# Graph attention on one core: exponentials behind a group's last round, the last head's products divided, four statistics in the MLP

## The chip, the cores and the metric

One core of a Trainium2 chip runs the whole program in one launch. The metric is the device time of one execution in microseconds (us); lower is better. The core has five engines with a queue of instructions each: TensorE (PE in the profile; PEld is its weight load), VectorE (DVE), ScalarE (ACT), GpSimd (POOL) and SyncE (SP, which issues loads). Each engine works off its queue in order and waits at semaphores for the others.

## The reference

The program computes a small transformer over a graph of 1250 nodes with 512 features, and then one graph aggregation:

```
for i in range(4):                          # layers
    y = cond_layer_norm(x, cond, s1, b1)    # (x-mu)*rsqrt(var+eps)*(1+scale)+bias, scale and bias from cond
    q, k, v = y@wq+bq, y@wk+bk, y@wv+bv     # 4 heads of 128
    scores = sum(q[src]*k[dst]); attn = softmax over the edges of each src
    x = x + (segment_sum(attn*v[dst], src) @ wo + bo)
    y = cond_layer_norm(x, cond, s2, b2)
    x = x + relu(y@m_w1+m_b1)@m_w2 + m_b2
x = layernorm(x0 + x)
x = layernorm(x + segment_sum(x[src]*edge_weight, dst) @ weight.T)
```

## The kernel before

The 1250 nodes are padded to NT = 10 tiles of 128. The edges are first turned into two dense tables of 10 x 128 x 1250: edge weights, and the logarithms of edge counts (an absent edge gets a huge negative value). Attention is then dense: for each head and each tile of 128 rows, scores against all 1250 nodes, plus the table's row (`Lr`, loaded by an issue of ScalarE's queue), then exp. Products in full precision are made of three matmuls each (`mm3`): operands are kept as a rounded high part and a low part, so each operand that is made on the way passes ScalarE, which writes the high part (`_hi`), and VectorE, which subtracts and writes the low part (`_lo`).

A layer is: normed and turned rows with queries, keys and values; attention, 4 heads h of GROUPS = 5 groups g of two tiles; the MLP, 5 chunks c of two tiles. Three layers run in a hardware loop, the fourth is written out behind it. There is no scheduler: in each engine's function `layer` the order of its work is written out by hand.

In group g of head h, all engines go through five rounds r:

- TensorE: `turn` transposes four 128x128 blocks of the two probability tiles (`prob`) into PSUM bank 5 or 6. Rounds 0 and 1 are the first tile's blocks 0 to 7, round 2 holds blocks 8 and 9 of both tiles, rounds 3 and 4 are the second tile's 0 to 7. Between the rounds stand the scores of the next group's two tiles (`scores_a`), the next head's queries and keys in a head's last group (`qk`), or, in the last head's last group, only two small conditioning products (`cond`). Also between rounds are the two output projections (`project`, j = 0 and 1) of the group before, at rounds 0 and 2.
- ScalarE: `pt_hi_` writes PT_hi of each round; `exp` of the next tiles; `o_hi_`.
- VectorE: `pt_lo_` writes PT_lo of each round; `mask` (i) adds the table to the scores of tile i and finds the maximum, at rounds 1 and at the end; `recip` (i) after exp (i); `add_wo` adds a projected tile to x; `o_lo_`.
- Before the rounds, TensorE does `out_heads` of the group before: the product of values and the turned probabilities, ten source tiles d of three matmuls, in the order 8, 9, 0 to 7, as PT_lo of rounds 2, 3 and 4 comes. It writes bank 7, from which `o_hi_` and `o_lo_` make the operand of `project`, which writes bank 7 too. `take_m` makes each next user of bank 7 wait for the one before: `out_heads` for the last `add_wo`, the second `project` for the first's `add_wo`.

A score's tile i = 10 h + 2 g + 2 is the first one of the next group, i - 1 the second one of this group. Transposes of round 0 wait for the exponential of a group's first tile, those of round 2 for its second. Transposes of round r also wait for PT_lo of round r - 2, for the bank.

The lines of the profile: L1479 the transposes, L1299 all `mm3` products (told apart by names: PT and v in `out_heads`, k and q in scores, wo and oT in `project`, mw in the MLP), L697 PT_hi, L1087 PT_lo, L1071 mask, L686 exp, L1077 and L1079 recip, L702 and L1091 `o_hi_` and `o_lo_`, L1101 `add_wo`. In the last group of the last head, VectorE also makes the first two normed tiles for the MLP: `center` (L1015) and `norm` (L1022). The statistics of each tile of x (`stats`, L1044 and L1047) are followed by `rsqrt` on GpSimd (L537, L539), and `norm` needs both.

Of the kernel before, what the change touches and what calls it, by code (L numbers as in the profile page):

```python
# [27 lines left out]
NT = -(-N // P)  # L28
# [4 lines left out]
H = 4  # L33
# [74 lines left out]
    o_ready=H * GROUPS, o_hi=H * GROUPS, o_split=H * GROUPS,  # L108
# [8 lines left out]
def build(nc, T, out):  # L117
    ctx = ExitStack()
    with ctx:
# [357 lines left out]
        def _(pool):  # L477
# [48 lines left out]
            def layer(l, ahead):  # L526
# [41 lines left out]
                for h in range(H):  # L568
                    for g in range(GROUPS):
# [3 lines left out]
                        if h == H - 1 and g:  # L573
                            rsqrt(NT + 2 * g - 2)
                            rsqrt(NT + 2 * g - 1)
                for n in range(2):
                    rest(MLP2 + n)
                rsqrt(2 * NT - 2)
                rsqrt(2 * NT - 1)
                for c in range(GROUPS):  # L580
                    h_rest(c, 0)
                    h_rest(c, 1)
                    if c == 0:
# [29 lines left out]
        def _(act):  # L613
# [48 lines left out]
            def layer(l, ahead):  # L662
# [28 lines left out]
                def pt_hi_(h, g, r):  # L691
                    n = (GROUPS * h + g) * 5 + r
                    wait("turned", n + 1)
                    if r == 0:
                        wait("o_ready", GROUPS * h + g)
# [52 lines left out]
                for h in range(H):  # L748
                    for g in range(GROUPS):
                        last, more = g == GROUPS - 1, h < H - 1  # L750
                        i = NT * h + 2 * g + 2
                        if g:
                            o_hi_(h, g - 1)
                            exp(i - 1)
                        for r in range(5):
                            pt_hi_(h, g, r)
                            if g == 0 and r == 0 and h:
# [3 lines left out]
                            if r == 2 and not last:  # L761
                                exp(i)
                            for n in pieces(h, g, r):
                                piece_hi(n)
                    if h < H - 1:
# [54 lines left out]
        def _(dve):  # L820
# [210 lines left out]
            def layer(l, ahead):  # L1031
# [100 lines left out]
                for h in range(H):  # L1132
                    for g in range(GROUPS):
                        last, more = g == GROUPS - 1, h < H - 1
                        i = NT * h + 2 * g + 2
                        if g:
                            o_lo_(h, g - 1)
                            recip(i - 1)
                        elif h:
                            mask(i - 1)  # L1140
                        for r in range(5):
                            pt_lo_(h, g, r)
                            if last and not more:
                                if r in (0, 3):
                                    center(NT + r // 3)
                                if r in (1, 4):
                                    norm(NT + r // 3)
                            if last and more:
# [3 lines left out]
                            if r in (0, 2):  # L1152
# [4 lines left out]
                            if r == 2 and not last:  # L1157
                                recip(i)
# [4 lines left out]
                        if g and not more:  # L1163
# [13 lines left out]
                for t in (NT - 2, NT - 1):  # L1177
                    stats(NT + t)
                for c in range(GROUPS):
                    if c < GROUPS - 1:  # L1180
                        for n in (NT + 2 * c + 2, NT + 2 * c + 3):
# [3 lines left out]
                            if n + 1 < 2 * NT:  # L1185
                                norm(n + 1)
                    elif ahead:
# [109 lines left out]
        def _(pe):  # L1297
# [108 lines left out]
            def layer(l, ahead):  # L1406
# [76 lines left out]
                def out_heads(h, g, parts):  # L1483
                    order = (8, 9, 0, 1, 2, 3, 4, 5, 6, 7)
                    if 0 in parts:
                        take_m("o_split", GROUPS * h + g + 1)
                    for d in [d for part in parts for d in order[5 * part:5 * part + 5]]:
# [4 lines left out]
                    if 1 in parts:  # L1492
                        m.then_inc(S["o_ready"], 1)

# [63 lines left out]
                for h in range(H):  # L1558
                    for g in range(GROUPS):
# [3 lines left out]
                        if g:  # L1563
                            out_heads(h, g - 1, (0, 1))
# [145 lines left out]
```

## Time and profile before

| what | before |
|---|---|
| median of 3 runs | 2042.48 us (2041.83 to 2045.47) |
| the profiled execution | 2040.49 us |
| its span, first to last instruction | 2038.7 us |
| granted TensorE clock, mean | 0.981 |
| TensorE matmuls busy | 1800.9 us, 88% |
| VectorE busy | 1332.7 us, 65% |
| ScalarE busy | 909.0 us, 45% |
| GpSimd busy | 391.5 us, 19% |

The span is what the trace covers; 1.8 us of the execution lie around it. Busy shares are means over the whole program. The rows that matter are those of single stretches. A timeline's row that ends in [x <-engine tile line] says that the engine stood idle for x us before it and what released it; neighbours on one engine overlap by some 0.1 us, so a step from start to start is a little shorter than the busy time.

### The profile page before, as it was taken

The page shows a single profiled execution, that of the slowest core. Times are in us where ns is not written, and L with a number is a line of the kernel's source. Part 1 is how long each engine was busy: PE and PEld are TensorE (multiplying, and loading weights), DVE is VectorE, ACT ScalarE, POOL GpSimd, SP SyncE. Part 2 cuts the span into 40 slices and gives each one's busy share as a digit, 9 for nine tenths or more (in the row PEclk, how much of TensorE's full clock was granted, in tenths as well). Part 3 has the DMA queues.
Part 4 walks back from the last instruction along what each step waited for, and adds up shares of the span by engine and source line. Part 5 has one row for each costly group of instructions (what it writes and reads, how often), then busy time and mean ns, then how long its engine had stood idle before and what let it go on. Part 6 is the DMA issues. An engine that isn't in the chain of part 4 may idle for free.

```text
span 2038.7 us, 35054 instructions
## 1 busy us (share of the span) xinstructions
PE 1800.9 (88%) x12603; PEld 1568.6 (77%) x12603; DVE 1332.7 (65%) x2447; ACT 909.0 (45%) x1525; POOL 391.5 (19%) x469
## 2 busy tenths in 40 slices
PE   1566359999999999999999999999999999999898
PEld 0455348988878789888787888887888988878777
DVE  8899955576685556766855567568555676685644
ACT  2798534454453244544532345445324454453221
POOL 5322223000024230000252200001523000023301
PEclk9999769999999999999999999999999999999999
DMA  1300352242231022432310224223101242232122
GB/s 23 108 0 0 135 202 78 77 140 87 84 122 46 17 67 85 133 96 82 118 52 16 66 87 130 88 88 122 53 15 58 85 136 93 81 121 88 38 66 73
DMA packets 62769, 165.95 MB, mean 81 GB/s; under 512 B 5777, under 2 KB 23986, under 8 KB 62605
## 3 DMA queue, kind: packets, MB, share of 16 engines
q10 hardware_dynamic: 23040, 102.41, 15.2%
q1 hardware_dynamic: 39572, 61.45, 9.6%
q8 instruction: 97, 1.59, 0.3%
q14 instruction: 60, 0.49, 0.1%
HBM read 146.58 MB, written 17.02 MB: 80 GB/s over the span
## 4 chain that ended last, share of the span: by engine, by line
PE 61%; issue 15%; DVE 13%; ACT 6%; DVEq 2%; DMA 1%; ACTq 1%; POOL 0%; POOLq 0%
PE ps L1299 55%; PE ps L1479 4%; DVE PT_lo L1087 3%; ACT PT_hi L697 3%; ACT prob L686 2%; PE ps L1401 2%; DVE prob L1071 2%; DVEq L934 1%; DVE CW L945 1%; DVE x L1101 1%; DVE CW L948 1%; DVE onehot L906 1%; DVE CW L992 1%; PE ps L1670 0%; DVE cpart L895 0%
## 5 line engine op out<-in xcount | busy, mean ns | idle before, releaser
L1087 DVE TENSOR_TENSOR PT_lo<-ps,PT_hi 128x512 fp32r<-128x512 f32 x400 | 271.1, 688 | 33.9 <-ACT PT_hi L697 17.0
L686 ACT ACTIVATE prob<-prob,nmax 128x1250 f32<-128x1250 f32 x160 | 214.2, 1338 | 176.6 <-DVE nmax L1071 176.6
L697 ACT ACTIVATE PT_hi<-ps 128x512 fp32r<-128x512 f32 x400 | 231.4, 590 | 69.3 <-PE ps L1479 69.2
L1479 PE MATMUL ps<-ident,prob 128*128 128x128 f32 x1600 | 244.1, 275 | 15.3 <-DVE PT_lo L1087 13.4
L1071 DVE CUSTOM_DVE_ANT_0 prob<-ps,Lr 128x1250 f32<-128x1250 f32 x160 | 232.5, 1453 | 35.5 <-PE ps L1299 31.8
L1299 PE MATMUL ps<-PT_hi,v_hi 128*128 128x256 f32 x800 | 233.0, 291 | 19.8 <-DVE PT_lo L1087 19.8
L1479 PEld LDWEIGHTS ps<-ident,prob 128*128 128x128 f32 x1600 | 182.7, 140 | 64.4 <-DVE PT_lo L1087 47.7
L1299 PE MATMUL ps<-PT_lo,v_hi 128*128 128x256 f32 x800 | 225.8, 282 | 0.0
L1299 PE MATMUL ps<-PT_hi,v_lo 128*128 128x256 f32 x800 | 225.7, 282 | 0.0
L1299 PE MATMUL ps<-k_hi,q_hi 128*128 128x512 f32 (+2 forms) x480 | 191.7, 399 | 0.5
L1299 PE MATMUL ps<-yT_hi,wqk_hi 128*128 128x256 f32 x640 | 184.7, 289 | 0.0
L1299 PE MATMUL ps<-yT_hi,wqk_lo 128*128 128x256 f32 x640 | 181.0, 283 | 0.0
L1299 PE MATMUL ps<-yT_lo,wqk_hi 128*128 128x256 f32 x640 | 180.8, 283 | 0.0
L1299 PEld LDWEIGHTS ps<-PT_hi,v_hi 128*128 128x128 f32 x800 | 152.4, 190 | 33.0 <-DVE PT_lo L1087 33.0
L1299 PE MATMUL ps<-k_lo,q_hi 128*128 128x512 f32 (+2 forms) x480 | 169.4, 353 | 0.0
L1299 PE MATMUL ps<-k_hi,q_lo 128*128 128x512 f32 (+2 forms) x480 | 169.4, 353 | 0.0
L1299 PE MATMUL ps<-win,onehot 128*128 128x128 bf16 x1680 | 105.7, 222 | 64.3 <-DVE CW L948 56.6
L1299 PEld LDWEIGHTS ps<-win,onehot 128*128 128x128 bf16 x1680 | 96.3, 99 | 74.5 <-DVE CW L948 65.9
L1299 PEld LDWEIGHTS ps<-PT_hi,v_lo 128*128 128x128 f32 x800 | 152.6, 191 | 0.0
L1299 PEld LDWEIGHTS ps<-PT_lo,v_hi 128*128 128x128 f32 x800 | 152.6, 191 | 0.0
L544 POOL TENSOR_TENSOR wo_lo<-piece,wo_hi 128x512 fp32r<-128x512 f32 x16 | 20.6, 1290 | 675.8 <-ACT wo_hi L728 675.8
L1053 DVE SCALAR_TENSOR_TENSOR q_lo<-ps,bias,q_hi 128x256 fp32r<-128x256 f32 x80 | 38.8, 484 | 148.2 <-ACT k_hi L676 148.2
(209 smaller groups left out, 4287.8 us busy)
## 6 DMA issues: line engine op xcount, KB each, us to landing
Lr<-l_table ACTq DMA_DIRECT2D x160, 625.0 KB, 3.8
piece<-in_L_gnn_m_w_dram SPq DMA_DIRECT2D x32, 256.0 KB, 2.7
w_table<-CW SPq DMA_DIRECT2D x1, 6250.0 KB, 17.7
l_table<-CW SPq DMA_DIRECT2D x10, 625.0 KB, 7.0
prob<-w_table SPq DMA_DIRECT2D x10, 625.0 KB, 3.9
x<-in_x_dram SPq DMA_DIRECT2D x2, 2304.0 KB
piece<-in_L_gnn_wv_dram SPq DMA_DIRECT2D x16, 256.0 KB, 2.8
piece<-in_L_gnn_wq_dram SPq DMA_DIRECT2D x16, 256.0 KB, 4.4
```

Of the source, the lines that this page charges most:

```text
L544: pool.tensor_tensor(lo, raw, hi.bitcast(F32), ALU.subtract).then_inc(S["piece_split"], 1)
L686: act.activation(buf, buf, ACT.Exp, bias=nmax[:, i % 4:i % 4 + 1], scale=-1.0, accum_out=rsum[:, i % 4:i % 4 + 1]).then_inc(S["exped"], 1)
L697: act.activation(o, i, ACT.Copy).then_inc(S["pt_hi"], 1)
L906: m = dve.tensor_scalar(onehot[:, j % SBUFS, b, :], iota_h[:], eT[:, 0, b, group], None, ALU.is_equal)
L934: base = dve.value_load(grow_i[0:1, bass.ds(i * UNROLL_G + j, 1)], min_val=0, max_val=N - WIN)
L945: dve.tensor_tensor(only, only, sums[:, 2], ALU.add).then_inc(e_chain, 1)
L1053: m = dve.scalar_tensor_tensor(out=lo[:, pair(c)], in0=bank(b, i * PAIR, (i + 1) * PAIR), scalar=bias[:, i, h:h + 1], in1=hi[:, pair(c)].b ...
L1071: dve.tensor_tensor_reduce(prob[:, i % 3, 0:N], ps[:, off:off + N], Lr[:, i % LBUFS, 0:N], -SCALE, BIG, ALU.add, ALU.min, nmax[:, i % 4:i ...
L1087: dve.tensor_tensor(lo, i, hi.bitcast(F32), ALU.subtract).then_inc(S["pt_split"], 1)
L1299: return pe.matmul(o, a, b, start=start, stop=stop)
L1401: m = pe.transpose(bank(5 + n % 2, k * P, (k + 1) * P), y[:, k * P:(k + 1) * P], ident[:])
L1479: m = pe.transpose(bank(5 + n % 2, at * P, (at + 1) * P), prob[:, (NT * h + 2 * g + j) % 3, d * P:(d + 1) * P], ident[:])
```

## The change

In an attention group, ScalarE's exponential of the next group's first tile moves from behind round 2 to behind round 4, and the exponential of the group's own second tile goes ahead of `o_hi_`. VectorE makes both reciprocals at the start of the group that uses the tiles, ahead of `o_lo_`. In the last group of the last head, `out_heads` of the group before is made in three parts, in the order 0 to 9, ahead of rounds 0, 1 and 2; a new semaphore, `o_part`, lets `pt_hi_` of rounds 0 and 1 overwrite what the first two parts have read. `o_hi_` and `o_lo_` then follow round 2, the projections follow rounds 2 and 3, and `add_wo` rounds 3 and 4. The statistics of the last four tiles of x, with their `rsqrt`, move from attention's end into the MLP's first two chunks. Elsewhere `out_heads` only takes its list of tiles in another form.

```diff
--- before.py
+++ after.py
@@ -105,7 +105,7 @@
     v_ready=NT, v_hi=NT, v_split=NT,
     scores_ready=H * NT, masked=H * NT, exped=H * NT, recip_ready=H * NT, 
     turned=H * GROUPS * 5, pt_hi=H * GROUPS * 5, pt_split=H * GROUPS * 5,
-    o_ready=H * GROUPS, o_hi=H * GROUPS, o_split=H * GROUPS,
+    o_ready=H * GROUPS, o_part=2, o_hi=H * GROUPS, o_split=H * GROUPS,
     wo_ready=H * NT, x_added=H * NT, bo_added=NT,
     bn_done=2 * NT, centered=2 * NT, inverted=H * NT, var_eps=2 * NT, h_ready=2 * GROUPS, h_relu=2 * GROUPS, h_split=2 * GROUPS,
     m2_ready=NT, x_mlp=NT,
@@ -570,16 +570,17 @@
                         for r in range(5):
                             for n in pieces(h, g, r):
                                 rest(n)
-                        if h == H - 1 and g:
+                        if h == H - 1 and 0 < g < GROUPS - 1:
                             rsqrt(NT + 2 * g - 2)
                             rsqrt(NT + 2 * g - 1)
                 for n in range(2):
                     rest(MLP2 + n)
-                rsqrt(2 * NT - 2)
-                rsqrt(2 * NT - 1)
                 for c in range(GROUPS):
                     h_rest(c, 0)
                     h_rest(c, 1)
+                    if c < 2:
+                        rsqrt(2 * NT - 4 + 2 * c)
+                        rsqrt(2 * NT - 3 + 2 * c)
                     if c == 0:
                         for n in range(2, KT):
                             rest(MLP2 + n)
@@ -691,7 +692,12 @@
                 def pt_hi_(h, g, r):
                     n = (GROUPS * h + g) * 5 + r
                     wait("turned", n + 1)
-                    if r == 0:
+                    if h == H - 1 and g == GROUPS - 1:
+                        if r < 2:
+                            wait("o_part", r + 1)
+                        elif r == 2:
+                            wait("o_ready", GROUPS * h + g)
+                    elif r == 0:
                         wait("o_ready", GROUPS * h + g)
                     o, i = round_view(PT_hi, n, r)
                     act.activation(o, i, ACT.Copy).then_inc(S["pt_hi"], 1)
@@ -750,18 +756,21 @@
                         last, more = g == GROUPS - 1, h < H - 1
                         i = NT * h + 2 * g + 2
                         if g:
-                            o_hi_(h, g - 1)
                             exp(i - 1)
+                            if more or not last:
+                                o_hi_(h, g - 1)
                         for r in range(5):
                             pt_hi_(h, g, r)
+                            if last and not more and r == 2:
+                                o_hi_(h, g - 1)
                             if g == 0 and r == 0 and h:
                                 exp(i - 1)
                             if last and more:
                                 qk_hi_(h + 1, r)
-                            if r == 2 and not last:
-                                exp(i)
                             for n in pieces(h, g, r):
                                 piece_hi(n)
+                        if not last:
+                            exp(i)
                     if h < H - 1:
                         exp(NT * (h + 1))
                         o_hi_(h, GROUPS - 1)
@@ -1134,8 +1143,10 @@
                         last, more = g == GROUPS - 1, h < H - 1
                         i = NT * h + 2 * g + 2
                         if g:
-                            o_lo_(h, g - 1)
+                            recip(i - 2)
                             recip(i - 1)
+                            if more or not last:
+                                o_lo_(h, g - 1)
                         elif h:
                             mask(i - 1)
                         for r in range(5):
@@ -1145,22 +1156,24 @@
                                     center(NT + r // 3)
                                 if r in (1, 4):
                                     norm(NT + r // 3)
+                                if r == 2:
+                                    o_lo_(h, g - 1)
+                                if r > 2:
+                                    add_wo(h, 2 * g - 5 + r)
                             if last and more:
                                 qk_lo_(h + 1, r)
                             if g == 0 and r == 1:
                                 recip(i - 1)
-                            if r in (0, 2):
+                            if r in (0, 2) and not (last and not more):
                                 if g:
                                     add_wo(h, 2 * g - 2 + r // 2)
                                 elif h:
                                     add_wo(h - 1, NT - 2 + r // 2)
-                            if r == 2 and not last:
-                                recip(i)
                             if r == 1 and not last:
                                 mask(i)
                         if not last:
                             mask(i + 1)
-                        if g and not more:
+                        if g and not last and not more:
                             stats(NT + 2 * g - 2)
                             stats(NT + 2 * g - 1)
                     if h < H - 1:
@@ -1174,8 +1187,6 @@
                 norm(NT + 2)
                 add_wo(H - 1, NT - 2)
                 add_wo(H - 1, NT - 1)
-                for t in (NT - 2, NT - 1):
-                    stats(NT + t)
                 for c in range(GROUPS):
                     if c < GROUPS - 1:
                         for n in (NT + 2 * c + 2, NT + 2 * c + 3):
@@ -1184,6 +1195,9 @@
                             y_lo_(n)
                             if n + 1 < 2 * NT:
                                 norm(n + 1)
+                        if c < 2:
+                            stats(2 * NT - 4 + 2 * c)
+                            stats(2 * NT - 3 + 2 * c)
                     elif ahead:
                         first(l + 1, 0)
                     if c:
@@ -1480,17 +1494,21 @@
                                          ident[:])
                     m.then_inc(S["turned"], 1)
 
-                def out_heads(h, g, parts):
-                    order = (8, 9, 0, 1, 2, 3, 4, 5, 6, 7)
-                    if 0 in parts:
+                ORDER = (8, 9, 0, 1, 2, 3, 4, 5, 6, 7)
+                FIRST, SECOND = ORDER[:5], ORDER[5:]
+
+                def out_heads(h, g, tiles, order=ORDER):
+                    if order[0] in tiles:
                         take_m("o_split", GROUPS * h + g + 1)
-                    for d in [d for part in parts for d in order[5 * part:5 * part + 5]]:
+                    for d in tiles:
                         if d in (8, 0, 4):
                             wait("pt_split", (GROUPS * h + g) * 5 + {8: 3, 0: 4, 4: 5}[d])
                         m = mm3(bank(7, 0, PAIR), v_hi[:, d, h * DH:(h + 1) * DH], v_lo[:, d, h * DH:(h + 1) * DH], PT_hi[:, d, :], PT_lo[:, d, :],
                                 d == order[0], d == order[-1])
-                    if 1 in parts:
+                    if order[-1] in tiles:
                         m.then_inc(S["o_ready"], 1)
+                    elif order is not ORDER:
+                        m.then_inc(S["o_part"], 1)
 
                 def project(h, g, j):
                     t = 2 * g + j
@@ -1560,11 +1578,14 @@
                         last, more = g == GROUPS - 1, h < H - 1
                         t = 2 * g + 2
                         before = (h, g - 1) if g else (h - 1, GROUPS - 1) if h else None
-                        if g:
-                            out_heads(h, g - 1, (0, 1))
+                        ending = last and not more
+                        if g and not ending:
+                            out_heads(h, g - 1, ORDER)
                         for r in range(5):
+                            if ending and r < 3:
+                                out_heads(h, g - 1, (range(4), range(4, 8), range(8, NT))[r], range(NT))
                             turn(h, g, r)
-                            if r == 2 and before:
+                            if r == (3 if ending else 2) and before:
                                 project(*before, 1)
                             if last and more:
                                 qk(h + 1, r)
@@ -1573,20 +1594,20 @@
                                     cond(NT + r // 2)
                             elif r != 2:
                                 scores_a(h, t + r // 3, r % 3)
-                            if r == 0 and before:
+                            if r == (2 if ending else 0) and before:
                                 project(*before, 0)
                     if more:
-                        out_heads(h, GROUPS - 1, (0,))
+                        out_heads(h, GROUPS - 1, FIRST)
                         wait("qk_split", GROUPS * (h + 2))
                         scores_a(h + 1, 0, 0)
                         scores_a(h + 1, 0, 1)
-                        out_heads(h, GROUPS - 1, (1,))
+                        out_heads(h, GROUPS - 1, SECOND)
                         scores_a(h + 1, 1, 0)
                         scores_a(h + 1, 1, 1)
                 turn_y(NT)
-                out_heads(H - 1, GROUPS - 1, (0,))
+                out_heads(H - 1, GROUPS - 1, FIRST)
                 turn_y(NT + 1)
-                out_heads(H - 1, GROUPS - 1, (1,))
+                out_heads(H - 1, GROUPS - 1, SECOND)
                 project(H - 1, GROUPS - 1, 0)
                 project(H - 1, GROUPS - 1, 1)
                 for c in range(GROUPS):
```

## Rows read from the trace of the kernel before

**Rows 1.** The page's first line.

```profile
span 2038.7 us, 35054 instructions
```

**Rows 2.** View of waits: who waited for whom, us in total, times, longest.

```profile
PE ps L1299 <- DVE PT_lo L1087: 19.8, 64, 0.3
```

**Rows 3.** Timeline of TensorE in a group: start us, us, instruction, [idle before <-releaser].

```profile
445.83 0.60 PE L1479 MATMUL ps<-ident,prob 128*128 128x128 f32 x4
...
449.82 0.66 PE L1479 MATMUL ps<-ident,prob 128*128 128x128 f32 x4
...
450.72 0.28 PE L1299 MATMUL ps<-PT_hi,v_hi 128*128 128x256 f32 x1
...
451.30 0.28 PE L1299 MATMUL ps<-PT_hi,v_lo 128*128 128x256 f32 x1
451.89 0.38 PE L1299 MATMUL ps<-PT_hi,v_hi 128*128 128x256 f32 x1 [0.31 <-DVE PT_lo L1087]
```

**Rows 4.** Timeline of VectorE in the same group.

```profile
447.10 0.69 DVE L1087 TENSOR_TENSOR PT_lo<-ps,PT_hi 128x512 fp32r<-128x512 f32 x1
447.70 1.45 DVE L1071 CUSTOM_DVE_ANT_0 prob<-ps,Lr 128x1250 f32<-128x1250 f32 x1
...
449.08 0.69 DVE L1087 TENSOR_TENSOR PT_lo<-ps,PT_hi 128x512 fp32r<-128x512 f32 x1
449.68 0.74 DVE L1101 SCALAR_TENSOR_TENSOR x<-ps,rnorm,x 128x512 f32<-128x512 f32 x1
450.66 0.16 DVE L1077 RECIPROCAL rinv<-rsum 128x1 f32<-128x1 f32 x1 [0.24 <-ACT prob L686]
...
451.14 1.29 DVE L1087 TENSOR_TENSOR PT_lo<-ps,PT_hi 128x512 fp32r<-128x512 f32 x2
```

**Rows 5.** Timeline of ScalarE in the same group and at the next one's start.

```profile
446.46 0.60 ACT L697 ACTIVATE PT_hi<-ps 128x512 fp32r<-128x512 f32 x1 [0.76 <-PE ps L1479]
...
449.20 1.34 ACT L686 ACTIVATE prob<-prob,nmax 128x1250 f32<-128x1250 f32 x1 [1.36 <-DVE nmax L1071]
...
455.06 0.38 ACT L702 ACTIVATE oT_hi<-ps 128x256 fp32r<-128x256 f32 x1 [3.46 <-PE ps L1299]
...
455.34 1.33 ACT L686 ACTIVATE prob<-prob,nmax 128x1250 f32<-128x1250 f32 x1
```

**Rows 6.** Timeline of TensorE, last group of the last head, first layer.

```profile
595.13 0.27 PE L1299 MATMUL ps<-PT_hi,v_hi 128*128 128x256 f32 x1
...
607.89 0.36 PE L1299 MATMUL ps<-PT_hi,v_hi 128*128 128x256 f32 x1
...
616.43 0.28 PE L1299 MATMUL ps<-yT_hi,mw_hi 128*128 128x256 f32 x1
```

**Rows 7.** Timeline of VectorE, the same group and the MLP's start.

```profile
602.31 0.74 DVE L1015 SCALAR_TENSOR_TENSOR y<-x,mv,ps 128x512 f32<-128x512 f32 x1
...
613.05 0.43 DVE L1091 TENSOR_TENSOR oT_lo<-ps,oT_hi 128x256 fp32r<-128x256 f32 x1 [0.69 <-ACT oT_hi L702]
...
617.29 0.69 DVE L1044 BATCH_NORM_STATS2 bn<-x 128x6 f32<-128x512 f32 x1
...
618.23 0.66 DVE L1044 BATCH_NORM_STATS2 bn<-x 128x6 f32<-128x512 f32 x1
```

**Rows 8.** Windows of TensorE, first and fourth layer: us, busy (x), clock, DMA, GB/s.

```profile
626.95:630.37 3.42, 3.42 (x18) 0.50 0.33 77
...
1850.50:1853.90 3.40, 3.37 (x26) 1.00 0.86 294
```

**Rows 9.** Timelines of GpSimd and VectorE in the MLP.

```profile
626.13 2.53 POOL L544 TENSOR_TENSOR mw_lo<-piece,mw_hi 128x512 fp32r<-128x512 f32 x2
632.47 1.30 POOL L552 TENSOR_TENSOR hT_lo<-h,hT_hi 128x512 fp32r<-128x512 f32 x1 [3.81 <-ACT hT_hi L714]
...
640.99 0.57 POOL L539 TENSOR_TENSOR rs<-rs,half 128x1 f32<-128x1 f32 x1
...
631.27 0.75 DVE L1015 SCALAR_TENSOR_TENSOR y<-x,mv,ps 128x512 f32<-128x512 f32 x1 [4.58 <-PE ps L1299]
```

## The prediction

> **What bounds the kernel now.** I read the page first: a span of 2038.7 us in an execution of 2040.49 us [rows 1]. TensorE (PE) is busy nearly everywhere in attention, so what can be won there is only what its waits cost, and an edit to ScalarE (ACT) or VectorE (DVE) counts only where it shortens or lengthens one of them. The view of waits has a striking entry: 64 waits of a matmul on the subtraction PT_lo, 0.3 us each, 19.8 us in all [rows 2]. 64 is four layers by four heads by four groups. The timeline of TensorE shows their place [rows 3]: `out_heads` issues six products for the source tiles 8 and 9, the sixth at 451.30, and the first for tile 0 at 451.89. Products of 256 columns otherwise follow each other by 0.12 us (450.72 to 451.30 is five steps), so the stall is 0.59 - 0.12 = 0.47 us; the view says 0.31 because it counts idle time from the modelled end of the last product.
>
> Who holds tile 0? It waits for round 3 of PT_lo, and the timelines of VectorE and ScalarE show why that is late [rows 4, 5]: the mask (447.70, 1.45 us) ends about 449.15, ScalarE starts the exponential at 449.20, and round 3's PT_hi, whose transposes were done long before, starts behind it, at about 450.5 (449.20 + 1.34). VectorE also sits in `recip`, which needs the same exponential (450.66, after 0.24 us idle), and reaches round 3 at 451.14. Its result is there at 451.83 and the product starts 0.06 us on.
>
> A second chain bounds the same group. Transposes of round 1 start at 445.83 and take 0.60 us to their end, PT_hi starts at 446.46 (0.60), PT_lo at 447.10, the mask at 447.70, PT_lo of round 2 at 449.08, ends 449.77, and round 4's transposes start at 449.82, 0.05 us later [rows 3, 4, 5]. So from round 1 to round 4 is 3.99 us, tied from link to link. Whatever is saved before round 1 shortens the group in full; whatever is saved after it, only up to round 4.
>
> **Part one, order of exponentials.** exp(i) moves from behind round 2 to behind round 4; exp(i-1) goes ahead of `o_hi`; the two recips move to the start of the next group. Nothing is added: the same number of instructions, DMA issues and waits. VectorE's new order in rounds 2 and 3 is PT_lo 449.08, `add_wo` 449.68, and, 0.66 us later (its busy 0.74 less the 0.08 by which neighbours overlap), PT_lo of round 3 at 450.34 to 451.03 [rows 4]. PT_hi of that round is free to run as soon as its transposes end. Tile 0 is wanted at 451.30 + 0.12 = 451.42, so the wait is over 0.33 us early and 0.47 us go. Does it come back? Behind round 4, ScalarE has exp(i) (1.34), then, when mask(i+1) is done, exp(i+1), and must be at `o_hi` when the products end. Let the first product be 0: round 4's transposes began at -0.90, PT_lo of round 4 ends about 1.1, mask(i+1) about 2.5, exp(i+1) about 3.9. The thirty products end at 3.85. That is level; before, `o_hi` came at 455.06 and exp(i+1) behind it at 455.34, 0.28 later, holding round 0 for 1.3 us [rows 5], and that hold now goes. The 0.66 us that `add_wo` needs lie before round 1's PT_hi is ready. The chain from round 1 to round 4 is as long as before, but starts 0.47 us earlier. In a head's first group exp(i-1) stays between rounds 0 and 1, and only the product stall goes. Of 64 stalls, 60 are in unchanged surroundings, 15 in each layer (the last head's last one belongs to part two): **60 x 0.47 = 28.2 us gained**. Bounds: 64 x 0.31 = 19.8, the view's own sum, and 64 x 0.47 = 30; I take the step between starts, because starts are what the next instruction goes by. The moved issues of Lr (one for each exponential) shift by 2 us and serve a mask two groups later, over 20 us away.
>
> **Part two, the last group of the last head.** Its `out_heads` is cut in three and put between transposes, and with it `o_hi`, `o_lo`, both `project` and both `add_wo` move: from rounds 0 and 2 to rounds 2, 3 and 4. The cost lies in what then waits for what. I walk it from the first product of the old order, 595.13 = 0 [rows 6], with durations of [rows 3, 4, 5, 7] (four transposes 0.60 to their end, PT_hi 0.60, PT_lo 0.60 to the next start, center, norm and `add_wo` 0.66 to the next start, o_lo 0.43):
> ScalarE: exp of the last tile runs 2.5 to 3.9, PT_hi of rounds 0 and 1 at 3.9 and 5.0. VectorE: mask until 2.4, two statistics (0.94 from one to the next) until 4.2, two recips (0.48 each, 450.66 to 451.14) until 5.2, PT_lo 5.2, center 5.8, PT_lo 6.5, norm 7.1, PT_lo 7.7, o_lo 8.35 to 8.8. TensorE: `project` 0 waits for o_lo: 8.85. Round 3's transposes stand behind it in TensorE's order: 9.6. Then PT_hi 10.25, PT_lo 10.9, center 11.5, `add_wo` 12.15 to 12.9. `project` 1 waits for that (one bank, 7): 12.95. Round 4's transposes stand behind it: 13.7. PT_hi 14.35, PT_lo 15.0, norm 15.6, `add_wo` 16.25 to 17.0. The last group's products need the same bank, so `take_m` holds them until 17.05. Before they started at 607.89, that is 12.76 [rows 6]. **Loss 17.05 - 12.76 = 4.3 us in each of four layers, 17.2 us.** Filling TensorE with the divided products saves nothing, since VectorE and the round trips set the pace; two serial loops through project and `add_wo` are new. What follows (o_lo 613.05, hidden layer at 616.43 [rows 6, 7]) waits as before and moves by as much. Bounds: 2.7 us if one of the two loops (project 1, 0.8, `add_wo` 0.66 and the wait of round 4 behind them) hides, 6 if the half clock below falls into it.
>
> **Part three, four statistics into the MLP.** 0.94 us each from start to start [rows 7]. Those of tiles 6 and 7 leave the ending, where they followed the critical norm and preceded an o_lo that waited for ScalarE anyway; those of tiles 8 and 9 ran at 617.29, where VectorE later idled. So removing them gains nothing. In the MLP, two go where VectorE has 4.58 us idle ahead of 631.27 [rows 9] and take 1.9. GpSimd's queue: `rsqrt` twice (a power of 0.57 each [rows 9], an addition and a wait before it; I take 0.9) now stands ahead of two weight subtractions, which started at 626.13 and ended at 628.66. VectorE is in reach of the two statistics from 626.6 and done at 628.5, `rsqrt` is done at 629.4, so the subtractions end about 632.0; the next thing on GpSimd started at 632.47, after 3.81 us idle [rows 9], and the pieces they pass on to SyncE's loads are wanted several us later. The two in the next step delay an MLP addition by at most their own 1.9 us, which the two output banks cover. Nothing, then; without this cover 1.9 us a layer, 7.5.
>
> **The clock.** In the first layer the MLP's second chunk ran 3.42 us at the half clock, 1.2 GHz, as it did in two more, and in the fourth at 2.4 [rows 8]; before each was an ending full of waits. Half the clock for 3.42 us costs up to 1.7 us; the new ending has more idle time, and I let the fourth layer fall too: +1.5. The Trainium skill, TensorE: Matmul & The Clock Gate, Part 1, has it that the throttled clock is the default and activity releases it. The trace agrees as far as these three stretches go; it doesn't show how much idle is enough. By this rule each of the longer endings falls once or more, and the sum is -9.5 or nearer to 0. By the rows alone the fourth layer could as well stay at full clock, and the sum would be -11.0.
>
> **Sum.** -28.2 + 17.2 + 1.5 = -9.5 us; 2040.49 becomes 2031.0. The median shown is 2042.48, 2.0 above the profiled execution, so the forecast is 2033.
>
> **Rivals.** (a) *The stall is exchanged for another.* Both exponentials now lie in the 3.85 us of the products, level with their end. If exp(i+1) is late by more than about 0.8 us, `project` 0, which waits for o_lo, stalls in every group. With all 28.2 us gone back, the ending's 17.2 + 1.5 stand alone: 2042.5 + 18.7 = 2061. It ends slower from the point where 0.24 us of each 0.47 return (14 of 28.2 us). For it: the slack at exp(i+1) is nil. Against: o_lo has 0.7 us of its own behind it. 0.12.
> (b) *The division works*, the ending loses nothing: 2042.5 - 28.2 = 2014. For it: TensorE's busy share in the old ending is low, so there are holes to fill. Against: the two loops above are in the program. 0.10.
> (c) *More half clock.* Two more stretches a layer than I count, at the ending and behind it: 4 x 2 x 1.5 = 12 more at most, half of that likelier: 2033 + 6 = 2039. For it: the new ending idles three times for over 2 us. Against: idle of this kind stood in the fourth layer too and the clock held [rows 8]. The Trainium skill's rule (same page) would by itself make it this case. 0.12.
> My forecast: 0.66.
>
> **Range and chances.** Forecast's own range, 2027 to 2039: the gain 24 to 30, the ending 3 to 6 a layer, the clock -4 to +6, not all at their ends. For 8 in 10 it opens to (c) and toward (b): 2022 to 2043. 0.2% is 4.1 us, about what a measurement of this kernel tells from no change: faster is below 2038.4. Forecast nearly all, (b), half of (c): faster 0.78; the rest of both: same 0.10; (a): slower 0.12.
>
> **What would show it.** The 64 waits of products on PT_lo go to near nothing; from first product to first product 11.08 us in place of 11.55, with 0.90 from round 4 to the first product as now [rows 3]; round 1 to round 4 stays 4.0. In the ending, `project` waits for oT_lo and then x, and the hidden layer starts 25.6 us after the first product in place of 21.3. I am wrong if `o_hi` stands waiting behind exp(i+1), or if the ending is no longer than it was.

## The result and the profile after

| | before | after |
|---|---|---|
| median of 5 runs | 2041.83 us (2040.37 to 2045.47) | 2031.72 us (2030.10 to 2034.29) |
| the profiled execution | 2040.49 us | 2034.29 us |
| its span | 2038.7 us | 2032.5 us |

The ratio is 0.9949, with a 95% interval of 0.9935 to 0.9962: 0.5% faster, 10.1 us by the medians. The profiled execution of the changed kernel is the slowest of its five, so its trace shows 6.2 us of them, not 10.1; why executions of one kernel differ by that much turns out to be part of the answer.

TensorE's timeline of a group after the change, the rows that answer to [rows 3] (here L1493 is the transposes, L1313 the products):

```profile
558.75 0.60 PE L1493 MATMUL ps<-ident,prob 128*128 128x128 f32 x4
...
562.74 0.66 PE L1493 MATMUL ps<-ident,prob 128*128 128x128 f32 x4
...
563.62 0.27 PE L1313 MATMUL ps<-PT_hi,v_hi 128*128 128x256 f32 x1
...
564.21 0.28 PE L1313 MATMUL ps<-PT_hi,v_lo 128*128 128x256 f32 x1
564.33 0.28 PE L1313 MATMUL ps<-PT_hi,v_hi 128*128 128x256 f32 x1
```

The sixth product at 564.21 is followed by the seventh 0.12 us later; the stall is gone. The view of waits has, in place of the 64 waits of [rows 2]:

```profile
PE ps L1313 <- DVE PT_lo L1096: 0.9, 4, 0.3
```

The four that are left stand in the four endings. From round 1 to round 4 it is 3.99 us as before. The first products of successive groups stand 10.98 us apart where it was 11.55. VectorE in the same groups, to compare with [rows 4]:

```profile
556.63 0.16 DVE L1086 RECIPROCAL rinv<-rsum 128x1 f32<-128x1 f32 x1 [1.23 <-ACT prob L687]
...
556.91 0.42 DVE L1100 TENSOR_TENSOR oT_lo<-ps,oT_hi 128x256 fp32r<-128x256 f32 x1
...
562.00 0.68 DVE L1096 TENSOR_TENSOR PT_lo<-ps,PT_hi 128x512 fp32r<-128x512 f32 x1
562.60 0.74 DVE L1110 SCALAR_TENSOR_TENSOR x<-ps,rnorm,x 128x512 f32<-128x512 f32 x1
563.26 1.50 DVE L1096 TENSOR_TENSOR PT_lo<-ps,PT_hi 128x512 fp32r<-128x512 f32 x2
```

Between rounds 2 and 3 there is only `add_wo` left, so round 3's PT_lo is there at 563.95, 0.4 us before it is wanted. The second reciprocal waits for its exponential and ends with the products. The ending tells the opposite story. TensorE, first layer, from the last score product to the hidden layer, against [rows 6]:

```profile
585.50 0.29 PE L1313 MATMUL ps<-k_hi,q_lo 128*128 128x286 f32 x1
...
594.10 0.64 PE L1313 MATMUL ps<-wo_hi,oT_hi 128*128 128x512 f32 x1 [0.42 <-DVE oT_lo L1100]
...
595.39 1.05 PE L1493 MATMUL ps<-ident,prob 128*128 128x128 f32 x4
599.17 0.80 PE L1313 MATMUL ps<-wo_hi,oT_hi 128*128 128x512 f32 x1 [2.73 <-DVE x L1110]
...
600.62 1.06 PE L1493 MATMUL ps<-ident,prob 128*128 128x128 f32 x4
...
604.40 0.58 PE L1313 MATMUL ps<-PT_hi,v_hi 128*128 128x256 f32 x1 [1.88 <-DVE x L1110]
...
614.49 0.28 PE L1313 MATMUL ps<-yT_hi,mw_hi 128*128 128x256 f32 x1
```

Each of the links that the prediction named is a row: the first projection waits for oT_lo, round 3's transposes stand behind it, the second projection waits for x, round 4's transposes stand behind that, and the last group's products wait for x again. From the last score to the hidden layer it is 29.0 us; before it was 21.4 (0.13 us more than from [rows 6], where the first row is the product behind that score). And the rows are slow in themselves: four transposes take 1.05 us here and 0.60 in the group above. The windows show the clock; the columns are us, TensorE busy with count, clock, DMA share, GB/s. The first four are the four endings, the next five the stretches at half clock inside them:

```profile
585.90:614.40 28.50, 19.97 (x106) 0.76 0.28 84
994.90:1023.10 28.20, 19.48 (x106) 0.82 0.29 84
1401.50:1430.00 28.50, 20.04 (x106) 0.76 0.27 84
1805.80:1832.20 26.40, 17.57 (x106) 0.94 0.30 94
```

```profile
594.24:607.89 13.65, 9.04 (x34) 0.50 0.21 60
1003.84:1010.67 6.83, 4.10 (x16) 0.50 0.26 73
1014.08:1017.49 3.41, 3.41 (x17) 0.50 0.16 62
1410.03:1423.68 13.65, 9.04 (x35) 0.50 0.20 59
1823.04:1826.45 3.41, 3.41 (x17) 0.50 0.20 76
```

Where the time went, by adding up such rows over the four layers of both traces (from the layer's first product of values and probabilities to the last head's last score; from there to the hidden layer; and all the rest):

| stretch | before | after | difference |
|---|---|---|---|
| attention up to the last score | 1005.1 | 971.2 | -33.9 |
| the four endings | 85.8 | 113.6 | +27.8 |
| everything else | 947.8 | 947.7 | -0.1 |
| span | 2038.7 | 2032.5 | -6.2 |

So the 10 us (6.2 in this execution) are what a gain of 34 leaves over a loss of 28.

### The profile page after: what moved, and what is told of

The parts are those of the page before. It is cut to its first block, busy times and chain, and to the rows that moved or that the text cites. A ratio compares the mean times of both kernels' runs of the same rounds, so it can differ in the third digit from the quotient of the medians.

```text
span 2032.5 us, 35060 instructions
## 1 busy us (share of the span) xinstructions
PE 1797.1 (88%) x12603; PEld 1571.1 (77%) x12603; DVE 1323.0 (65%) x2447; ACT 922.6 (45%) x1525; POOL 391.2 (19%) x469
## 4 chain that ended last, share of the span: by engine, by line
PE 76%; DVE 11%; issue 8%; ACT 2%; DVEq 2%; DMA 1%; POOL 0%; ACTq 0%; SPq 0%; POOLq 0%
PE ps L1313 65%; PE ps L1493 8%; PE ps L1415 2%; DVE PT_lo L1096 1%; DVEq L943 1%; DVE prob L1080 1%; DVE CW L954 1%; DVE CW L957 1%; ACT PT_hi L703 1%; DVE onehot L915 1%; DVE CW L1001 1%; PE ps L1691 0%; ACT prob L687 0%; DVE x L1110 0%; DVE cpart L904 0%
## 5 line engine op out<-in xcount | busy, mean ns | idle before, releaser
L703 ACT ACTIVATE PT_hi<-ps 128x512 fp32r<-128x512 f32 x400 | 239.1, 598 | 270.6 <-PE ps L1493 270.4
L1493 PE MATMUL ps<-ident,prob 128*128 128x128 f32 x1600 | 250.0, 279 | 13.2 <-DVE PT_lo L1096 11.1
L1493 PEld LDWEIGHTS ps<-ident,prob 128*128 128x128 f32 x1600 | 183.1, 142 | 74.1 <-DVE PT_lo L1096 57.5
L1313 PE MATMUL ps<-PT_hi,v_hi 128*128 128x256 f32 x800 | 230.4, 288 | 9.0 <-DVE x L1110 8.1
L1313 PE MATMUL ps<-PT_hi,v_lo 128*128 128x256 f32 x800 | 228.1, 285 | 0.0
L1313 PE MATMUL ps<-PT_lo,v_hi 128*128 128x256 f32 x800 | 228.0, 285 | 0.0
L1313 PE MATMUL ps<-k_hi,q_hi 128*128 128x512 f32 (+2 forms) x480 | 191.6, 399 | 0.5
L1313 PE MATMUL ps<-yT_hi,wqk_hi 128*128 128x256 f32 x640 | 184.7, 289 | 0.0
L1313 PE MATMUL ps<-yT_hi,wqk_lo 128*128 128x256 f32 x640 | 180.9, 283 | 0.0
L1313 PE MATMUL ps<-yT_lo,wqk_hi 128*128 128x256 f32 x640 | 180.8, 283 | 0.0
L1313 PE MATMUL ps<-k_hi,q_lo 128*128 128x512 f32 (+2 forms) x480 | 169.6, 353 | 0.0
L1313 PE MATMUL ps<-k_lo,q_hi 128*128 128x512 f32 (+2 forms) x480 | 169.2, 352 | 0.0
L1313 PEld LDWEIGHTS ps<-PT_hi,v_hi 128*128 128x128 f32 x800 | 154.9, 194 | 11.6 <-DVE x L1110 9.4
L1313 PE MATMUL ps<-win,onehot 128*128 128x128 bf16 x1680 | 104.7, 221 | 65.1 <-DVE CW L957 57.4
L1313 PEld LDWEIGHTS ps<-PT_hi,v_lo 128*128 128x128 f32 x800 | 155.1, 194 | 0.0
L1313 PEld LDWEIGHTS ps<-PT_lo,v_hi 128*128 128x128 f32 x800 | 154.9, 194 | 0.1
L1313 PEld LDWEIGHTS ps<-win,onehot 128*128 128x128 bf16 x1680 | 95.3, 99 | 75.2 <-DVE CW L957 66.6
L1110 DVE SCALAR_TENSOR_TENSOR x<-ps,rnorm,x 128x512 f32<-128x512 f32 x160 | 119.3, 746 | 40.2 <-PE ps L1313 39.9
```

The costliest lines, as they stand in the source:

```text
L703: act.activation(o, i, ACT.Copy).then_inc(S["pt_hi"], 1)
L1110: dve.scalar_tensor_tensor(out=x[:, t, :], in0=bank(7), scalar=rnorm[:, i % 8:i % 8 + 1], in1=x[:, t, :], op0=ALU.mult, op1=ALU.add).then_ ...
L1313: return pe.matmul(o, a, b, start=start, stop=stop)
L1493: m = pe.transpose(bank(5 + n % 2, at * P, (at + 1) * P), prob[:, (NT * h + 2 * g + j) % 3, d * P:(d + 1) * P], ident[:])
```

## The experiments

Ratios are to runs of the kernel before on the same chip, whose median was 2040.7 to 2041.6 us in each set; a difference between medians of two sets can be off by about that 1 us.

**1. The order of exponentials alone.** On the kernel before, ScalarE's and VectorE's order in the groups as in the change, nothing else:

```diff
                         if g:
-                            o_hi_(h, g - 1)
                             exp(i - 1)
+                            o_hi_(h, g - 1)
...
-                            if r == 2 and not last:
-                                exp(i)
                             for n in pieces(h, g, r):
                                 piece_hi(n)
+                        if not last:
+                            exp(i)
...
                         if g:
-                            o_lo_(h, g - 1)
+                            recip(i - 2)
                             recip(i - 1)
+                            o_lo_(h, g - 1)
...
-                            if r == 2 and not last:
-                                recip(i)
```

> Theory (order of exponentials gains, ending loses): the distance from one group's first product to the next falls from 11.55 to 10.98 us as in the changed kernel, 60 times, and the last group of the last head gains its stall too: 34 us or a little more, 2041.8 becomes 2005 to 2009. Rival (the whole change gains 10 us because each part gains little and the ending loses nothing): 2030 to 2035.

Measured 2002.60 us, ratio 0.9807 (0.9794 to 0.9821): 39 us faster, 2.4 us beyond the range expected. Its trace has groups of 10.98 us, attention up to the last score of 242 to 243 us a layer (34.3 us less in four), and endings of 20.3 to 21.0 us in place of 21.4 (3.3 us less). The first ending, TensorE:

```profile
585.64 0.28 PE L1298 MATMUL ps<-PT_hi,v_hi 128*128 128x256 f32 x1
...
605.84 0.28 PE L1298 MATMUL ps<-yT_hi,mw_hi 128*128 128x256 f32 x1
```

20.2 us against the 21.3 of [rows 6]. Of the 1.1 us between them, 0.57 is the stall of [rows 3] once more: each layer's sixteenth stands behind the last score, so inside the ending. The theory stands and the rival falls.

**2. The ending alone.** On the kernel before, `out_heads` in three parts, `o_part`, and the moved `o_hi`, `o_lo`, `project` and `add_wo`:

```diff
...
+                            if ending and r < 3:
+                                out_heads(h, g - 1, (range(4), range(4, 8), range(8, NT))[r], range(NT))
                             turn(h, g, r)
-                            if r == 2 and before:
+                            if r == (3 if ending else 2) and before:
                                 project(*before, 1)
...
-                            if r == 0 and before:
+                            if r == (2 if ending else 0) and before:
                                 project(*before, 0)
...
```

> Theory: the ending alone, on the old order of exponentials, is 4 us longer in each layer at full clock, and up to 7.5 where half clock falls into it: 16 to 30 us slower, 2058 to 2072. Groups stay at 11.55. Rival (the division as such fills holes and the loss in the changed kernel comes from the new order of exponentials): no slower than 2042.

Measured 2064.60 us, ratio 1.0115 (1.0100 to 1.0131): 23 us slower. Endings are 26.6 to 29.1 us in place of 21.4. The new ending costs by itself, with the old order of exponentials around it too. Which part of it costs, the division or the loops behind it, is experiment 5's question.

**3. The statistics alone.** On the kernel before, four `stats` and their `rsqrt` moved into the MLP:

```diff
...
-                for t in (NT - 2, NT - 1):
-                    stats(NT + t)
...
+                        if c < 2:
+                            stats(2 * NT - 4 + 2 * c)
+                            stats(2 * NT - 3 + 2 * c)
```

> Theory: VectorE waits around both places, so nothing, 2038 to 2046. Rival (the statistics hold VectorE in the ending): up to 1.9 us a layer faster, 2034. Rival (GpSimd's queue is late for the MLP): 2 us a layer slower, 2050.

Measured 2041.01 us, ratio 0.9999 (0.9990 to 1.0008): nothing.

**4. The change without its ending.** Experiments 1 and 3 together.

> The changed kernel with its ending undone. Theory: the whole of the exponentials' gain, nothing of the ending's loss: 2004 to 2009, about 25 us faster than the changed kernel, and equal to the order of exponentials alone. Rival (the statistics' move pays only with the divided products): 2012 or more.

Measured 2002.49 us, ratio 0.9806 (0.9793 to 0.9819): the same as the exponentials alone.

**5. The two loops opened.** In the changed kernel, the products stay divided, but both projections go behind the transposes of the next round:

```diff
-                            if r == (3 if ending else 2) and before:
+                            if r == (4 if ending else 2) and before:
                                 project(*before, 1)
...
-                                if r in (0, 2):
-                                    cond(NT + r // 2)
+                                if r in (0, 3):
+                                    cond(NT + r // 3)
...
-                            if r == (2 if ending else 0) and before:
+                            if r == (3 if ending else 0) and before:
                                 project(*before, 0)
```

> The changed kernel with both projections of the last group but one issued behind the transposes of rounds 3 and 4 instead of between them (and the second conditioning product behind round 3). Theory (two serial loops through project and add_wo set the ending's loss): the loops open, the last group's products start about 13 us behind the old first product in place of 16.7, and the loss shrinks to near zero at full clock: 2004 to 2012. Rival (dividing the products in itself costs, PT_hi waiting for o_part): 2025 or more.

Measured 2005.52 us, ratio 0.9818 (0.9802 to 0.9835), 26 us faster than the changed kernel. TensorE in the first ending:

```profile
593.23 0.66 PE L1493 MATMUL ps<-ident,prob 128*128 128x128 f32 x4 [0.60 <-DVE PT_lo L1096]
...
594.90 0.47 PE L1313 MATMUL ps<-wo_hi,oT_hi 128*128 128x512 f32 x1 [0.42 <-DVE oT_lo L1100]
...
595.68 0.60 PE L1493 MATMUL ps<-ident,prob 128*128 128x128 f32 x4
...
596.73 0.50 PE L1313 MATMUL ps<-wo_hi,oT_hi 128*128 128x512 f32 x1 [0.45 <-DVE x L1110]
```

Round 3's transposes now go ahead of the first projection and round 4's ahead of the second, which waits 0.45 us for x where it waited 2.73. The last group's products start 12.7 us behind the last score in place of 18.9, and endings are 21.3 to 21.9 us. Against experiment 4's endings (20.4 to 21.0) the divided products cost 1.0 us a layer in the mean and gain nothing; in experiment 4 the last group's products start 11.8 us behind the last score. The loops, with the half clock in the endings that they bring, cost the rest.

**6. Half clock taken out.** The changed kernel with 22 products of 512 columns more in each layer's ending, issued into a bank that nobody reads then: 4 ahead of the wait for y (1.25 us), 10 ahead of the second projection's (2.73) and 8 ahead of the last group's (1.88). Their results are not used; the kernel does more work than the reference needs.

```diff
+                def fill(n):
+                    for _ in range(n):
+                        mm(bank(4), cstack[:, nt(0)], stacks[:, MB2_AT, :], True, True)
...
+                            if ending and r == 3:
+                                fill(10)
...
```

> The changed kernel with 22 products of 512 columns in each layer's ending whose results nobody reads, issued ahead of TensorE's waits. Theory (12 of the ending's 28 us are half clock): the clock holds at 2.4 GHz in the endings, each is about 25.4 us from last score to hidden layer in place of 27 to 29, the chain itself stays: 2017 to 2024. Rival (the ending's loss is the chain alone, the half clock falls into waits): 2030 or more.

Measured 2020.38 us, ratio 0.9900 (0.9883 to 0.9916): 11 us faster than the changed kernel, by adding work. The windows of its four endings:

```profile
586.20:611.10 24.90, 20.76 (x128) 1.00 0.32 97
991.20:1016.10 24.90, 20.79 (x128) 1.00 0.32 97
1394.20:1419.10 24.90, 20.71 (x128) 1.00 0.34 97
1793.30:1818.20 24.90, 20.73 (x128) 1.00 0.33 96
```

The clock holds, and every ending is 25.4 us from the last score. The added products don't lengthen the chain, since TensorE still waits behind them:

```profile
594.36 0.47 PE L1313 MATMUL ps<-wo_hi,oT_hi 128*128 128x512 f32 x1 [0.42 <-DVE oT_lo L1100]
...
598.45 0.50 PE L1313 MATMUL ps<-wo_hi,oT_hi 128*128 128x512 f32 x1 [0.57 <-DVE x L1110]
...
602.58 0.38 PE L1313 MATMUL ps<-PT_hi,v_hi 128*128 128x256 f32 x1 [0.56 <-DVE x L1110]
```

So the chain costs 25.4 - 21.4 = 4.0 us a layer, 15.8 in all, and half clock the other 12.0 of the 27.8. The two profiled executions are 16.2 us apart: beside these 12.0, the stretches at half clock that followed the third and the fourth ending (at 1440.75 and 1843.52 in the changed kernel) are not there either, and the time outside attention and endings is 3.8 us shorter.

**7. Which part of the new order.** The changed kernel with `o_hi` and `o_lo` ahead of exp(i-1) and its recip again:

```diff
                         if g:
-                            exp(i - 1)
                             if more or not last:
                                 o_hi_(h, g - 1)
+                            exp(i - 1)
...
```

> The changed kernel with o_hi and o_lo ahead of exp(i-1) again, as before the change; exp(i) stays behind round 4. Theory (only the product stall mattered; the hold of round 0's PT_hi lies beside other work): groups stay near 10.98, same as the changed kernel, 2028 to 2036. Rival (the swap is half of the gain): groups of 11.2 or more, 2043 or more.

Measured 2031.07 us, ratio 0.9950 (0.9934 to 0.9967), the same as the changed kernel, and groups of 10.97 to 10.99 us. ScalarE in a group:

```profile
563.77 0.60 ACT L703 ACTIVATE PT_hi<-ps 128x512 fp32r<-128x512 f32 x1 [1.33 <-PE ps L1493]
...
564.26 1.34 ACT L687 ACTIVATE prob<-prob,nmax 128x1250 f32<-128x1250 f32 x1
...
567.74 0.38 ACT L708 ACTIVATE oT_hi<-ps 128x256 fp32r<-128x256 f32 x1 [2.06 <-PE ps L1313]
...
568.02 1.33 ACT L687 ACTIVATE prob<-prob,nmax 128x1250 f32<-128x1250 f32 x1
...
569.34 0.59 ACT L703 ACTIVATE PT_hi<-ps 128x512 fp32r<-128x512 f32 x1
```

The exponential holds round 0's PT_hi for 1.3 us again, and it costs nothing. On VectorE round 0's PT_lo now starts 4.6 us ahead of round 3's where it was 5.8 in the changed kernel, but round 1's, the next link of the chain, 3.25 us ahead in both. The groups' gain comes from exp(i) and its recip, moved from behind round 2; exp(i) and recip(i) were not moved apart from each other.

**8. A version that beats all of these.** Experiment 4, and the MLP's first hidden products ahead of the last two projections, the second of them behind the first `turn_y`:

```diff
-                project(H - 1, GROUPS - 1, 0)
-                project(H - 1, GROUPS - 1, 1)
                 for c in range(GROUPS):
                     hidden(c, 0)
+                    if c == 0:
+                        project(H - 1, GROUPS - 1, 0)
                     if c < GROUPS - 1:
                         turn_y(NT + 2 * c + 2)
+                    if c == 0:
+                        project(H - 1, GROUPS - 1, 1)
                     hidden(c, 1)
```

> The kernel with the new order of exponentials, the statistics in the MLP and the old ending, and now the MLP's first half chunk of hidden products ahead of the last two projections. Theory (at the end of attention TensorE stands still 1.2 us for o_lo and 1.2 us for add_wo, while the hidden products' operands are ready): both waits go beside the 24 hidden products, 2.0 to 2.5 us a layer, 2002.5 becomes 1992 to 1995. Rival (the wait for y, transposed behind the hidden products, only comes later by as much): 2000 or more.

Measured 1987.88 us, ratio 0.9739 (0.9726 to 0.9752), 14.6 us faster than experiment 4 where 8 to 10 were expected (13.7 by the two ratios, which were measured on different chips). TensorE at the place where experiment 4 idles twice:

```profile
602.51 0.28 PE L1300 MATMUL ps<-PT_hi,v_lo 128*128 128x256 f32 x1
602.63 0.28 PE L1300 MATMUL ps<-yT_hi,mw_hi 128*128 128x256 f32 x1
...
605.51 0.40 PE L1300 MATMUL ps<-wo_hi,oT_hi 128*128 128x512 f32 x1
...
607.22 0.50 PE L1300 MATMUL ps<-wo_hi,oT_hi 128*128 128x512 f32 x1
...
608.01 0.28 PE L1300 MATMUL ps<-yT_hi,mw_hi 128*128 128x256 f32 x1
```

And the same place in experiment 4:

```profile
602.81 0.28 PE L1300 MATMUL ps<-PT_hi,v_lo 128*128 128x256 f32 x1
604.12 0.47 PE L1300 MATMUL ps<-wo_hi,oT_hi 128*128 128x512 f32 x1 [1.02 <-DVE oT_lo L1092]
...
606.13 0.50 PE L1300 MATMUL ps<-wo_hi,oT_hi 128*128 128x512 f32 x1 [1.07 <-DVE x L1102]
...
606.97 0.41 PE L1300 MATMUL ps<-yT_hi,mw_hi 128*128 128x256 f32 x1
```

Both waits are gone, 2.4 us a layer or 9.8. The last row starts a hidden chunk at half clock (0.41 us for a product in place of 0.28); in its trace experiment 4 has four stretches of 3.4 us at half clock around here in three layers, and experiment 8 has none. At about 1.4 us each (the 24 products of a half chunk took 4.20 us from first to last start there and 2.76 in experiment 8) that is about the 5 us missing. That the shorter waits are what kept the clock up was argued from the two traces, not tried apart.

## Why the prediction was right, point by point

Forecast 2033, measured 2031.7, in the likeliest case and inside its own range. The mechanism was right in both main parts. That the sum came within 2 us is in part luck: two of its three terms lay outside the bounds given for them (24 to 30 for the gain, -4 to +6 for the clock), and their errors have opposite signs.

**The order of exponentials: mechanism right, size too small.** The stall was between the sixth and seventh product, its cause exp(i) ahead of round 3, and it did not come back. The second chain, round 1 to round 4, was as long as walked, 3.99 us. The term was 60 x 0.47 = 28.2; measured 60 x 0.57 = 34, and 33.9 in the trace. The sign was the distance from first product to first product, forecast 11.08 and measured 10.98. What I left out stands one row below the last of [rows 3], in the kernel before:

```profile
451.89 0.38 PE L1299 MATMUL ps<-PT_hi,v_hi 128*128 128x256 f32 x1 [0.31 <-DVE PT_lo L1087]
452.11 0.28 PE L1299 MATMUL ps<-PT_lo,v_hi 128*128 128x256 f32 x1
```

After a wait the first product takes 0.22 us to the next start and not 0.12. A stall's price is the wait and the slow first instruction behind it: 0.47 + 0.10. (The first product behind transposes is as slow without any wait: 0.36 us at 607.89 in [rows 6] for 0.28.) The swap of exp(i-1) and `o_hi`, which frees round 0's PT_hi, was given no price of its own, rightly (experiment 7). With the new order the old ending gets 0.8 us shorter as well (experiment 1): 0.57 is its own stall, the rest stays open.

**The ending: right.** Walked: 4.3 us a layer; measured at full clock 4.0 (experiment 6), 15.8 for 17.2. The walk put project 0, project 1 and the last group's products at 8.85, 12.95 and 17.05, so 4.10 us for each of the two loops; in experiment 6 they start at 594.36, 598.45 and 602.58, so 4.09 and 4.13. The two loops are the cause (experiment 5), and the division fills no hole that mattered. Rival (b), 2014, falls with experiment 2.

**The statistics: right**, nothing (experiments 3 and 4).

**The clock: too small.** I had +1.5 us. The endings alone hold 12.0 us of it in the profiled execution. The text called the ending's idle time longer and then let one stretch fall, in the fourth layer's MLP. That one came (1843.52), but the second layer's went, so the stretches just behind the endings are three as before; what was added lies inside the endings, at 40.95 us of half clock in all. Rival (c) had this mechanism, and its bound of 12 us more is about what the profiled execution shows: with the gain no larger than forecast the sum would have come to 2038 to 2042, near this case's 2039. The Trainium skill, TensorE: Matmul & The Clock Gate, Part 1, says that a throttled clock is the default and activity releases it. All four endings fell, as the prediction had it by this rule, and experiment 6 agrees: 22 idle products a layer brought the windows from 0.76, 0.82, 0.76 and 0.94 to 1.00, and 11 us. The spread goes the same way: the five executions of the changed kernel had mean clocks of 0.971 to 0.974, the slowest (2034.3 us, the profiled one) the lowest and the fastest (2030.1) the highest.

Together: in the profiled execution the gain was 5.7 us more than forecast, the chain 1.4 less and the clock's loss 10.5 more, -33.9 + 15.8 + 12.0 = -6.1. By the medians the change is -10.1; if gain and chain were the same there, some 8 us are left for the clock, an estimate, and the errors nearly cancel (-9.5 forecast). By parts: the order of exponentials gains 39 us alone (experiment 1), and the new ending costs 29 on top of it (2031.72 against 2002.49 in experiment 4). Rival (a), an exchanged stall, fell: the second exponential is level with the products' end and `o_hi` starts with it, which costs nothing.

## What to carry to other kernels

A stall that repeats inside a dense stream of matmuls, here 60 times, is worth removing, and its price is the wait plus a slow first instruction; but first ask which chain between engines runs beside it. Here the stall lay ahead of that chain, which stayed at 3.99 us, and so came off in full, while a hold of 1.3 us beside other work cost nothing (experiment 7). Work that is put between rounds to fill holes brings its waits along: in an in-order queue a projection that waits for another engine also holds the transposes that this other engine waits for, and such a loop costs more than the hole it fills. If an edit adds waits to TensorE, count half clock too; putting independent products ahead of the wait (here the MLP's hidden products) took away the waits, 9.8 us, and by the traces half clock behind them as well.

## What the runs showed of the hardware

A mean clock of 0.97 to 0.98 hides what the clock does in one stretch. In the changed kernel's first ending the granted clock fell to 0.50, its lower level of 1.2 GHz, at 594.24, right behind waits of 1.25 and 0.42 us, and stayed there for 13.65 us, through waits of 2.73 and 1.88; no wait of this ending before the fall was longer than 1.25 us. Products that nobody needs, put ahead of the waits, held the clock at 1.00 and made the program 11 us faster. And a matmul behind a wait takes 0.1 us longer to the next start, even at full clock (0.22 against 0.12).
